# A two-image kernel on one core: when buffers are cleared, when gathers are issued, and how the tail of the grams is cut

## What is computed

```
x = x + attention(gn(x))     # 1x1 conv to q,k,v; 3x3 depthwise; 24x24 attention per head; 1x1 conv
x = x + motif(gn(x))
# gn: normalise over (H, W, 3 channels), 32 groups
```

```
gram = einsum('bgjcl,bgjdl->bgjcd', motif, motif)
d2   = sq[..., :, None] + sq[..., None, :] - 2*gram;  d2 = where(eye, inf, d2)
nn   = argmin(d2, -1);  u_max = max(nn, -1);  c_max = sum(nn == u_max)
term = floor(motif * motif[u_max] * c_max / 8)
out  = sum over the nine shifts of (motif * (b != 0) + term), each at its shift
```

## Time and profile before

| | us |
|---|---|
| runs shown (3) | 1780.07, 1781.23, 1782.25; median 1781.23 |
| profiled execution: its own time | 1786.56 |
| profiled execution: span | 1784.6 |
| busy in the span: PE, DVE, ACT, POOL | 1497.0, 990.3, 735.0, 317.9 |

### The profile page before, as it was taken

How to read it: one execution, slowest core, us unless ns; L and a number is a source line. 1 busy time by engine, 2 the same in 40 slices (tenths; PEclk the granted TensorE clock), 3 DMA queues, 4 the chain that set the end, 5 groups by cost and what they waited for, 6 DMA issues and landing times. The chain is left out here.

```text
span 1784.6 us, 40475 instructions
## 1 busy us (share of the span) xinstructions
PE 1497.0 (84%) x16955; PEld 1257.2 (70%) x16955; DVE 990.3 (55%) x1537; ACT 735.0 (41%) x769; POOL 317.9 (18%) x254
## 2 busy tenths in 40 slices
PE   0699999799299488988949999988975993898998
PEld 0699999699299344544539999988974991454554
DVE  7333332123743379999962333321346415999998
ACT  0133332100154178877812332330003532888886
POOL 2222222000531202100022222220005302024000
PEclk9999999899699689999979999998996996999999
DMA  5111111010003364462112222201010216362511
GB/s 190 35 35 34 37 35 28 13 74 38 36 2 143 116 234 166 151 215 74 38 63 60 61 60 59 61 16 49 38 73 1 85 61 234 99 198 78 169 59 52
DMA packets 50959, 145.99 MB, mean 82 GB/s; under 512 B 12311, under 2 KB 33421, under 8 KB 48143
## 3 DMA queue, kind: packets, MB, share of 16 engines
q1 hardware_dynamic: 46192, 116.10, 20.4%
q0 software_dynamic: 4608, 27.49, 4.3%
HBM read 72.69 MB, written 37.75 MB: 62 GB/s over the span
## 5 line engine op out<-in xcount | busy, mean ns | idle before, releaser
L1301 PE MATMUL acc<-rnd,ident 128*128 128x376 f32 x1152 | 405.5, 497 | 24.7 <-ACT rnd L1284 24.7
L599 PE MATMUL ps_a<-wa,xa 128*128 128x192 f16 x2304 | 406.2, 248 | 14.0 <-DMA xc<-low 14.0
L600 PE MATMUL ps_a<-wb,xb 128*128 128x192 f16 x2304 | 405.6, 248 | 0.0
L1301 PEld LDWEIGHTS acc<-rnd,ident 128*128 128x128 f32 x1152 | 224.6, 199 | 153.1 <-ACT rnd L1284 26.1
L1279 ACT ACTIVATE rnd_m<-prod,plus_round,scale 128x1504 f32<-128x1504 f32 x144 | 236.0, 1639 | 121.2 <-DVE prod L1097 114.8
L1097 DVE TENSOR_TENSOR prod<-fc,near 128x1504 f32<-128x1504 f32 x144 | 246.6, 1713 | 39.5 <-DMA near<-near 25.2
L1213 DVE SCALAR_TENSOR_TENSOR over<-prod,scale,rnd 128x1504 bf16<-128x1504 f32 x144 | 255.4, 1776 | 0.9 <-PE acc L1305 0.9
L599 PEld LDWEIGHTS ps_a<-wa,xa 128*128 128x128 f16 x2304 | 227.0, 99 | 15.5 <-issue 11.7
L468 DVE TENSOR_TENSOR qk<-ps_a,qk 128x384 f16<-128x384 f32 x128 | 71.4, 557 | 295.4 <-ACT squares L549 295.4
L1284 ACT ACTIVATE rnd<-rnd_m,minus_round 128x1504 f32<-128x1504 f32 x144 | 223.1, 1550 | 25.9 <-PE acc L1305 20.8
L600 PEld LDWEIGHTS ps_a<-wb,xb 128*128 128x128 f16 x2304 | 227.3, 99 | 1.0
(11 more groups left out here) (227 smaller groups left out, 2030.1 us busy)
## 6 DMA issues: line engine op xcount, KB each, us to landing
x_planes<-img SPq DMA_DIRECT2D x8, 1536.0 KB, 5.6
f_planes<-img SPq DMA_DIRECT2D x8, 1536.0 KB, 11.1
fc<-f_planes SPq DMA_DIRECT2D x16, 768.0 KB, 4.6
x1c<-x_planes SPq DMA_DIRECT2D x16, 768.0 KB, 4.8
out<-x1c SPq DMA_DIRECT2D x16, 768.0 KB, 3.3
near<-near SPq DMA_DIRECT2D x96, 107.9 KB, 2.2
xb<-xa SPq DMA_DIRECT2D x64, 97.5 KB, 2.1
img<-in_x SPq DMA_DIRECT2D x4, 1536.0 KB, 12.6
```

What stands on the lines that cost most here:

```text
L599: nc.tensor.matmul(out, xa[:, row, dx:dx + W], wa[:, t, :], start=(t == 0), stop=False)
L600: nc.tensor.matmul(out, xb[:, row, dx:dx + W], wb[:, t, :], start=False, stop=False)
L1301: nc.tensor.matmul(o(m), k["ident"][:, :], rnd[:, n % RNDS, BR * m:BR * m + BR, :], start=False, stop=False, skip_group_check=True)
```

## The change

In `prepare`, tables are made once: `second_block` and `first_part` carry the factor 1/8, `iota_less` is iota minus 8, `own_big` is the diagonal times 1e30, and `row_base` the eight slabs' first offsets. In `attention`, POOL waits for `stat_ready` 2 before its first clearing. In `motif_grams` the clearings of `turned_hi` and `turned_lo` go, but for eight columns behind `turned_hi`; the gram products read 126 partitions instead of 128; the waits for `cleared` move from the copies to PE's first transpose. The two last blocks are accumulated for groups 0 to 7 and then for 8 to 15, with a second semaphore, and copied out and reordered in those halves; DVE masks and reduces each third straight from PE's banks; and several small steps go (the row constant of the distances, two products with constants, the shift by 8 back, the factor 1/8). In `motif_terms` the index takes one instruction instead of nine, each gather from slab 2 on waits for the product of the step in whose place it stands, and `x1c` of slabs 0 and 1 is loaded at shift 2.

```diff
@@ attention
         def _(pool):
 
+            pool.wait_ge(stat_ready, 2)
             nc.gpsimd.memset(low[:].rearrange("p s y x -> p (s y x)").bitcast(U32), 0).then_inc(ones_made, 1)
@@ motif_grams
             for s in range(2):
-                nc.gpsimd.memset(split[s][:, :, W:XP, :].rearrange("p h x c -> p h (x c)"), 0.0)
-                nc.gpsimd.memset(turned_hi[s][:].bitcast(U32), 0)
-                nc.gpsimd.memset(turned_lo[s][:].bitcast(U32), 0).then_inc(cleared, 1)
+                nc.gpsimd.memset(split[s][:, :, W:XP, :].rearrange("p h x c -> p h (x c)"), 0.0).then_inc(cleared, 1)
+                nc.gpsimd.memset(turned_hi[s][0:HM, TCOLS:TCOLS + MC], 0.0).then_inc(cleared, 1)
...
-            act.wait_ge(chunk_done, C // CHUNK)
-            for j in range(2):
-                last = nc.scalar.activation(g_half[:, 4 * j:4 * j + 4, :], acc[j][0:CW, 0:4 * CW]
...
+            for j in (0, 2):
+                act.wait_ge(chunk_done, C // CHUNK + j // 2)
+                nc.scalar.activation(g_half[:, 4 * j:4 * j + 4, :], acc[j][0:CW, 0:4 * CW]
+                                     .rearrange("p (g r) -> p g r", r=CW), ACT.Copy
+                                     ).then_inc(gram_out2 if j == 2 else gram_out, 1)
...
-                                                turned_hi[s][:, a:a + P], t[:, a:a + CW], start=False, stop=False,
+                                                turned_hi[s][0:HM, a:a + P], t[0:HM, a:a + CW], start=False, stop=False,
...
-            while m < BLOCKS:
-                gram(m)
-                m += 1
-
-            pe.wait_ge(gram_out, 2)
+            for side in range(2):
+                for m_ in range(m, BLOCKS):
+                    gram(m_, range(8 * side, 8 * side + 8))
+
             for g in range(MG):
+                if g in (0, 8):
+                    pe.wait_ge(gram_out if g == 0 else gram_out2, 2)
...
-            dve.wait_ge(post_act, 6)
-            c.then_wait(nc.vector.tensor_tensor(g_all[:], g_all[:], k["same_block"][:, :].unsqueeze(1)
-                                                .to_broadcast([MR, MG, MR]), ALU.mult))
-            c.then_wait(nc.vector.tensor_reduce(blk[:], g_all[:].rearrange("p g (j d) -> p g d j", d=MC), X,
-                                                ALU.add))
+            for j in range(3):
+                n = min(PER, MG - PER * j)
+                third = slice(PER * j, PER * j + n)
+                dve.wait_ge(post_pe, 3 + j + 1)
+                c.then_wait(nc.vector.tensor_tensor(
+                    g_all[:, third, :], ps_t[j][0:MR, 0:n * MR].rearrange("p (g r) -> p g r", r=MR),
+                    k["same_block"][:, :].unsqueeze(1).to_broadcast([MR, n, MR]), ALU.mult))
+                last = nc.vector.tensor_reduce(blk[:, third, :], g_all[:, third, :]
+                                               .rearrange("p g (j d) -> p g d j", d=MC), X, ALU.add)
+            c.then_wait(last)
@@ motif_terms
-                if sh == 1 and i < 2:
+                if sh == 2 and i < 2:
                     load_rows(x1c, x1_dram, i, x1_in)
...
-                    if sh == 1 and i >= 2:
-                        product_made(pool, number[(i - 2, KK - 1)])
-                        product_made(pool, number[(i - 2, KK - 2)])
+                    product_made(pool, n)
...
-            for i in range(N):
-                last = nc.vector.tensor_scalar(index_f[:, :, i], offset[:, :], k["group_base"][:, 0:1],
-                                               float(first_row(i) * C), ALU.add, ALU.add)
-            c.then_wait(last)
-            nc.vector.tensor_copy(index[:], index_f[:]).then_inc(indexed, 1)
+            nc.vector.tensor_tensor(index[:], offset[:, :].unsqueeze(2).to_broadcast([P, 2, N]),
+                                    k["row_base"][:, :].unsqueeze(1).to_broadcast([P, 2, N]), ALU.add
+                                    ).then_inc(indexed, 1)
```

More of the change, by code:

```diff
@@ L824, in _ @@
                     high(u // PER_PIECE + 2)
-            act.wait_ge(chunk_done, C // CHUNK)
-            for j in range(2):
-                last = nc.scalar.activation(g_half[:, 4 * j:4 * j + 4, :], acc[j][0:CW, 0:4 * CW]
-                                            .rearrange("p (g r) -> p g r", r=CW), ACT.Copy)
-            last.then_inc(gram_out, 1)
-            for step, dst in enumerate((g_turn, g_all)):
-                for j in range(3):
-                    n = min(PER, MG - PER * j)
-                    act.wait_ge(post_pe, 3 * step + j + 1)
-                    nc.scalar.activation(dst[:, PER * j:PER * j + n, :],
-                                         ps_t[j][0:MR, 0:n * MR].rearrange("p (g r) -> p g r", r=MR),
-                                         ACT.Copy).then_inc(post_act, 1)
+            for j in (0, 2):
[5 more added lines that the diff above has]
+                n = min(PER, MG - PER * j)
+                act.wait_ge(post_pe, j + 1)
+                nc.scalar.activation(g_turn[:, PER * j:PER * j + n, :],
+                                     ps_t[j][0:MR, 0:n * MR].rearrange("p (g r) -> p g r", r=MR),
+                                     ACT.Copy).then_inc(post_act, 1)
         @block.tensor
@@ L863, in first_need, with gram @@
                 return min(3 * m + 5, CHUNK * q + COLS - 1, C - 1) // 2
-            def gram(m):
+            def gram(m, groups=range(MG)):
                 q = min(m // 8, 3)
                 s, at = q % 2, 3 * m - CHUNK * q
+                last = None
                 pe.wait_ge(out_hi, first_need(m) + 1)
                 pe.wait_ge(out_lo, first_need(m) + 1)
-                for g in range(MG):
+                for g in groups:
                     a = (g * COLS + at) * CK
@@ L973, in _ @@
-            c.then_wait(nc.vector.tensor_reduce(blk[:], g_all[:].rearrange("p g (j d) -> p g d j", d=MC), X,
-                                                ALU.add))
+            for j in (1, 3):
+                dve.wait_ge(chunk_done, C // CHUNK + j // 2)
+                nc.vector.tensor_copy(g_half[:, 4 * j:4 * j + 4, :], acc[j][0:CW, 0:4 * CW]
+                                      .rearrange("p (g r) -> p g r", r=CW)).then_inc(gram_out2 if j == 3 else gram_out, 1)
+            for j in range(3):
+                n = min(PER, MG - PER * j)
+                third = slice(PER * j, PER * j + n)
[5 more added lines that the diff above has]
+                                               .rearrange("p g (j d) -> p g d j", d=MC), X, ALU.add)
```

73 lines of the change are left out of this document (36 added, 37 removed).

## The result

The changed kernel takes **1729.22 us** (median of 4 runs, 1727.61 to 1730.13) where the kernel before takes 1780.65 in the same series (4 runs, 1779.73 to 1782.25): ratio 0.9708, 95% interval 0.9696 to 0.9720, 51.4 us less. The forecast was 71.5 us less, 1709.7, with a range of 1699 to 1726. The direction was right and the size was not. The profiled execution of the changed kernel spans 1727.1 us and took 1728.85.

A forecast was written before the change was run, and what follows sets the result against it. PE's holes were put down to DVE statistics held by POOL's clearings, the grams' tail chain, and products waiting for SP's moves. Terms 13.2 + 27.8 + 10.8 + 1.2 + 18.5 = 71.5 us off 1781.2 gave 1709.7, range 1699 to 1726.

The forecast's parts named there:

- POOL later in attention: Start of attention: DVE's small statistics steps no longer held by POOL's clearings; 7.2 us in image 0, 6.0 in image 1.
- clearings dropped: Grams' statistics: DVE steps held beside POOL's clearings fall to 0.18 us each; 13.8 us in image 0, 14.0 in image 1.
- halves and thirds: Tail of the grams: PE's gap gone, 1.4 us an image, and masking and reduction overlapped with PE, 2.3 an image.
- fewer small steps: Tail of the grams: seven small steps go and some become narrower; 1.7 us an image.
- index: Start of the terms: eight index instructions and a cast become one, first gather leaves earlier; 0.6 us an image.
- gathers and `x1c`: Terms: fewer transfers beside the moves; 8 us in image 0, 7 in image 1, 3.5 at image 1's product 42.
- the last term: The terms' gathers and `x1c` loads issued later so that moves land sooner; 18.5 us, bounds 0 and 22.
- The rule that I set against the row: GpSimd contends with DVE instructions in a 2-port mode or with two SBUF inputs; L91, two inputs, showed only 0.50 us.
- the lower of my two bounds: Index saving at the start of the terms: between 0 and 1.2 us an image arrive; the lower is 0.
- Rival 2: Terms: moves stay slow because of `x1c`, image 1's rows and paced gathers; last term about 4 us, 1724 us; 13%.
- Rivals 1, 3 and 4: Two-input steps held by delayed clearings, 1723 (9%); late gathers, 1782 to 1792 (2%); clearings not holding small steps, 1751 (2%).

## Why the prediction missed

| step | forecast | measured |
|---|---|---|
| POOL later in attention | 13.2 | 13.2 by the runs, 12.3 by the stages |
| clearings dropped | 27.8 | 26.8 by the runs, 28.6 by the stages |
| halves and thirds | 7.4 | 9.8 by the runs, 9.5 by the stages |
| fewer small steps | 3.4 | 3.8 by the timeline, not run alone |
| index | 1.2 | nothing that shows, not run alone |
| gathers and `x1c` | 18.5 | -1.8 by the runs |

"By the runs" is the difference of medians to the changed kernel's 1729.22, which stands in another series. By the ratios to the kernel before of each series, the runs give 13.4, 25.5, 8.7 and -2.1 us in place of 13.2, 26.8, 9.8 and -1.8; no conclusion changes.

The kernel with everything but the last term gains 54.7 us (1782.12 in its series to 1727.46, ratio 0.9696) against 53.0 forecast for the first five terms.

*The clearings.* Right in mechanism and size. Tensor-scalars and copies with both ends in on-chip memory are held and two-input steps are not. I read the second from L91 and L110, and it held for L477 too. L110 was no evidence: it starts at 51.40, when POOL's last clearing of that series (L408, 0.92 us from 50.29) has ended. L108 would have been, with two inputs and 0.19 us from 50.95. The rule that I set against the row was the less exact of two: the Trainium skill (SBUF — State Buffer, "Who interferes with whom") says that a step with two on-chip inputs contends with a GpSimd instruction that reads on-chip memory, not with one that only writes it. A clearing only writes, and the trace agrees: L477 at 1.41 us for two beside the 6.49 us clearing, L98 at 0.50 beside those of 4.27.

*Halves.* Mechanism right, the term 2.4 us too small in all; of the 4.7 us an image by the stages, 4.0 are found in the tail.

*Small steps.* From the step behind the reduction to the end of the stage it was 9.38 us (599.79 to 609.17) and is 7.62 (574.25 to 581.87): 1.76 in image 0. In image 1 it was 9.37 and is 7.30, 2.07. Forecast 1.7 each.

*Index.* POOL's first gather leaves 0.75 us after the stage's start instead of 1.84, but product 0 starts 9.35 us after it instead of 9.18. It waits for the gather's landing (8.58 us of wait instead of 7.23), and that did not come earlier: the lower of my two bounds.

*Gathers and `x1c`: the step that failed.* The step of the prediction was: product 4 comes at 13.8 us "after product 0 instead of 22.4: 8.6, less something for the gathers of slabs 2 and 3, which now fall beside the moves of steps 5 to 8: 8". The first half was right (13.15). The "something", which I put at 0.6 us, was 7.7: of 9.3 us that image 0 had gained at product 4, 1.5 were left at the end of the pair. In image 1 it was 8.1 at product 4 (21.47 to 13.41, forecast 7) and 4.6 at the end. What took it back was a gather and a 768 KB load that leave within 0.3 us of each other and hold the next move. I had moved the gathers and the `x1c` loads separately and never laid POOL's wait (product n) and SP's (product n-2) on one axis; the kernel's text gives it, and the timeline shows 0.3 us between them. And I gave the pacing no cost in the later pairs, where a burst around a pair's start had held no product. It cost 2.8 and 1.7 us in image 0 and 2.0 in image 1. The 3.5 us for product 42 were read from an event that half of the executions have. Rival 2 named the mechanism, "`x1c`, the next image's rows and the paced gathers that hold them", at 13% and with 4 us left of the term; even that was too much. My evidence against it, that the pitch before was 3.34 "with the same loads in flight", held for loads but not for gathers: before, POOL had issued its last gather at 621.19, and product 5 starts at 644.11. The sign that I had named for being wrong, "a move of 6 us and more at the start of the terms", came: 6.9 us in the median.

Also in the working: the profiled execution of before lay 5.3 us above its median, and I took the difference off the total but kept terms that were part of it. And the range does not follow from its parts: halves and index at their worst and half of the 18.5 us are 14.3 up, not 12, and the best cases are 6.9 down, not 10. Only the lower bound that the term itself had, 0, reaches the measured time; the range took half of it.

Rivals 1, 3 and 4 did not come: no held two-input step; DVE waited for a gather only at the first two products of each image, so none was late at a pair's boundary; and the clearings do hold the small steps (the two runs that brought them back).

The fastest kernel of the study is the changed one with its gathers at shifts 2 and 6, 1713.61 us. That this is within 4 us of my 1709.7 does not bear the forecast out: it is another kernel, and even there the last term is worth 13.9 us (1727.46 to 1713.61) and not 18.5, while halves and thirds gave more than I had put.

## What to carry to other kernels

When an issue is paced by progress on one queue, list what every other queue issues at the same progress, with each loop's lead taken off (here two products), and check that the smallest urgent transfer still lands within its slack beside whatever leaves with it. Two edits can undo each other: here the kernel was 7.8 us faster without the one, 3.6 without the other, and no faster without both than the 1.8 us that hardly stand out. And before a gap in one profile becomes a term, look whether a second profile of the same kernel has it.

## What was not expected of the hardware

- At the same mean rate (8.4 to 8.6 MB in 34 us) a 108 KB move lands in 6.9 us in the median where a gather and a 768 KB load leave 0.3 us apart, and in 2.4 or 4.0 where they leave 2.8 us and more apart (gathers moved, or SP's loads moved); the first of these two windows holds half as many bytes of gathers. `fc`'s loads went from 4.6 to 8.0 us and the stores from 3.3 to 5.5 in the changed kernel, and are at 5.0 and 3.3 with the gathers at shifts 2 and 6.
- POOL's issue of an indirect gather beside DVE's products takes 0.94 to 3.88 us, but now and then 15.57, at one place of the program (the first gather of image 1's last burst) in three of six profiles of kernels with bursts, and always the same length. What sets it was not tried.
- Where DVE's held steps stand against POOL's clearings varies between executions (7.60, 2.57, 4.20 or 11.86, 2.53, 0.18) while their sum does not (14.4 and 14.6 us).
